# One core: the keys of a node lookup are turned on TensorE with the slots, and the marks of a tile lie in a run

## The chip, the cores and the metric

The kernel runs on one core of one Trainium2 chip. The metric is the device time of one execution in microseconds (us), the median of several runs. In the text PE is TensorE, DVE is VectorE, ACT is ScalarE, POOL is GpSimd and SP is SyncE, which here only issues DMAs.

## The reference

One layer of a graph network, with a normalisation behind it. There are 12,500 nodes with 32 features and 400,000 edges sorted by their destination.

```python
msg = jax.nn.relu(node_inputs[src] + edge_inputs)
agg = jax.ops.segment_sum(msg, dst, num_segments=N_NODES)
h = (1.0 + eps[0]) * node_inputs + agg
y = h @ W.T + b
x = _layernorm(x + y, axis=-1)
```

The costly part is `node_inputs[src]`: 400,000 rows of 32 floats, read at random places.

## The kernel before, in words

The edges are cut into 195 batches of 2048 (and a short first one). A batch is 16 tiles of 128 edges. The rows of its 8 first tiles are fetched by POOL with indirect DMAs (`gather_tile`, L536), one for each tile of 128 rows. The rows of the other 8 tiles are looked up on TensorE, in two stages, with the node table `xparts` held in SBUF as three bf16 parts.

- First lookup (`look_in_buckets`, L1154, tile `l`): a node's low bits are its bucket (32), the rest its place. Each source gets a slot in its bucket. Marks `oh1` (1 where a slot's place is the lane) are made by DVE (L754, two of three) and ACT (L989, L996) from `slots`, a row of 1824 numbers that every partition gets by a broadcast DMA. ACT copies the result to `table` (L964).
- Second lookup (`look_in_table`, L1173, tile `found`): marks `oh2` say which slot each of the 1024 edges wants. They are made from `keys`, 1024 numbers broadcast in the same way, by DVE (L766, three of four blocks) and ACT (L1008, L1014). A step does 4 blocks x 8 tiles x 3 parts = 96 matmuls of 128x128, each with 128 columns of marks as its weights. The marks stand edge by edge, tiles innermost, and `PITCH` is LOOK + 2 = 10, so the 128 marks of one tile lie 10 elements (20 bytes) apart.

Then DVE picks the right row out of `found` (L781), adds the edge's features for all 16 tiles (`add_rows`, L797), ACT does the relu (L979), DVE marks each edge's node in a window of 40 (L800), PE sums (L1184), and DVE adds the window to `aggX` (L824).

How slots and keys come about, for the batch two steps ahead: DVE marks buckets (L703), PE counts ranks (`count_ranks`, L1205, L1207, L1211 with the contiguous weights `before` and `ones`), DVE takes the rank (L717, L725), the key (`give_key`, L740) and the placement (L733, L745). PE fills the slots (`fill_slots`, L1220: 8 matmuls into 32 partitions of `ranks`), ACT copies them to `slot_row` (L971). SP writes key and slots to DRAM (L483, L489) and reads both back, spread over all partitions (L491, L497).

Each engine runs its own program. Nothing is scheduled: the order is that of the `step` functions, and semaphores join them. In step s PE does `look_in_buckets`, the sums of batch s-1, blocks 0 and 1 of `found`, `fill_slots` for s+2, block 2, `count_ranks` for s+3, block 3. POOL gathers batch s+3 in three turns; each turn waits until PE has come far enough in step s (`l1_ready`, `blocks_looked`), so POOL may be some two steps ahead of `add_rows`, but no more. SP's order in a step is index, key write, edges, slot write, key broadcast, slot broadcast; a wait there holds up all that is behind it.

## Time and profile before

| | |
|---|---|
| median of 3 runs | 2077.78 us (2077.75 to 2079.56) |
| the profiled execution, its own time | 2076.23 us |
| its span (first to last instruction) | 2074.0 us |
| mean granted TensorE clock | 0.995 of full |
| PE busy | 2012.9 us (97%) |
| DVE, ACT, POOL busy | 80%, 76%, 73% |
| `found` (L1173), PE busy | 1241.0 us, 18720 matmuls |
| gathers (L536), POOL busy | 1517.0 us, 1565 gathers |

Matmuls are pipelined: a row of the timeline that holds n of them lasts n - 1 intervals and the whole length of the last. A POOL row is POOL's own part of one gather; when the gathered rows have landed is not in it. The time between two rows of one engine that the trace puts down to nothing is called "issue". Busy shares are averages over the run.

### The profile page before, as it was taken

The page shows a single profiled execution, that of the slowest core. Times are in us where ns is not written, and L with a number is a line of the kernel's source. Part 1 is how long each engine was busy: PE and PEld are TensorE (multiplying, and loading weights), DVE is VectorE, ACT ScalarE, POOL GpSimd, SP SyncE. Part 2 cuts the span into 40 slices and gives each one's busy share as a digit, 9 for nine tenths or more (in the row PEclk, how much of TensorE's full clock was granted, in tenths as well). Part 3 has the DMA queues.
Part 4 walks back from the last instruction along what each step waited for, and adds up shares of the span by engine and source line. Part 5 has one row for each costly group of instructions (what it writes and reads, how often), then busy time and mean ns, then how long its engine had stood idle before and what let it go on. Part 6 is the DMA issues. An engine that isn't in the chain of part 4 may idle for free. (4 is left out here: it accounts for less than half of the span.)

```text
span 2074.0 us, 117127 instructions
## 1 busy us (share of the span) xinstructions
PE 2012.9 (97%) x46449; PEld 1920.2 (93%) x46449; DVE 1649.0 (80%) x4231; ACT 1566.4 (76%) x1616; POOL 1517.5 (73%) x1571
## 2 busy tenths in 40 slices
PE   2999999999999999999999999999999999999997
PEld 2899999999999999999999999999999999999994
DVE  6888888878888888877888888877888888887885
ACT  5777777777777777777777777777777777777774
POOL 6477777777777777777777777777777777777770
PEclk9999999999999999999999999999999999999998
DMA  6344444444544444444444444444444444444441
GB/s 157 86 112 109 110 111 110 113 114 115 112 111 110 110 111 110 114 112 112 116 111 110 110 110 111 114 113 112 115 112 110 109 110 111 111 115 112 115 112 35
DMA packets 236283, 228.68 MB, mean 110 GB/s; under 512 B 104218, under 2 KB 185556, under 8 KB 236062
## 3 DMA queue, kind: packets, MB, share of 16 engines
q1 hardware_dynamic: 183023, 200.99, 33.5%
q0 software_dynamic: 50080, 25.74, 12.7%
q10 hardware_dynamic: 3154, 1.60, 0.4%
q8 instruction: 17, 0.28, 0.1%
q14 instruction: 9, 0.07, 0.0%
HBM read 225.43 MB, written 2.71 MB: 110 GB/s over the span
## 5 line engine op out<-in xcount | busy, mean ns | idle before, releaser
L536 POOL DMA_INDIRECT rows_all<-in_x,index x1565 | 1517.0, 969 | 507.1 <-issue 474.0
L1173 PE MATMUL found<-table,oh 128*128 128x128 bf16 x18720 | 1241.0, 225 | 11.4 <-issue 3.1
L1173 PEld LDWEIGHTS found<-table,oh 128*128 128x128 bf16 x18720 | 1167.9, 144 | 43.6 <-issue 21.2
L1008 ACT ACTIVATE oh<-keys,minus_lanes 128x1024 bf16<-128x1024 f16 x195 | 224.2, 1150 | 310.3 <-PE found L1173 294.4
L1154 PE MATMUL l<-xparts,oh 128*57 128x96 bf16 x18720 | 436.5, 207 | 0.9 <-ACT oh L996 0.9
L1154 PEld LDWEIGHTS l<-xparts,oh 128*57 128x57 bf16 x18720 | 409.7, 108 | 14.1 <-issue 1.1
L989 ACT ACTIVATE oh<-slots,minus_lanes 128x1824 bf16<-128x1824 f16 x195 | 351.3, 1801 | 0.0
L781 DVE COPY_PREDICATED rows_all<-mask,found 128x256 f32<-128x256 uint16 x780 | 343.3, 440 | 7.6 <-issue 1.4
L964 ACT CAST table<-l 128x768 bf16<-128x768 f32 x390 | 311.1, 798 | 40.2 <-PE l L1154 26.0
L996 ACT ACTIVATE oh<-oh 128x1824 bf16<-128x1824 bf16 x195 | 335.7, 1721 | 0.0
L775 DVE TENSOR_TENSOR mask<-iota,side 128x32 f16<-128x32 f16 x195 | 37.6, 193 | 305.2 <-PE found L1173 290.1
L766 DVE TENSOR_SCALAR oh<-keys,lanes 128x1024 bf16<-128x1024 f16 x585 | 274.2, 495 | 1.1 <-PE found L1173 1.0
L754 DVE TENSOR_SCALAR oh<-slots,lanes 128x1824 bf16<-128x1824 f16 x390 | 272.5, 740 | 0.2 <-DMA slots<-slot_dram 0.2
L1184 PE MATMUL win<-onehots,relus 128*32 128x40 f32 x6250 | 238.1, 204 | 3.5 <-DVE aggX L824 3.3
L1184 PEld LDWEIGHTS win<-onehots,relus 128*32 128x32 f32 x6250 | 214.3, 112 | 17.4 <-DVE aggX L824 4.2
L1014 ACT ACTIVATE oh<-oh 128x1024 bf16<-128x1024 bf16 x195 | 206.9, 1061 | 0.0
L979 ACT ACTIVATE relus<-msg 128x512 f32<-128x512 f32 (+1 forms) x196 | 123.7, 631 | 94.8 <-DVE msg L797 94.8
L800 DVE TENSOR_TENSOR onehots<-win,rel 128x640 f32<-128x640 f32 (+1 forms) x196 | 157.3, 803 | 0.0
L797 DVE TENSOR_TENSOR msg<-rows_all,msg 128x512 f32<-128x512 f32 (+1 forms) x196 | 133.1, 679 | 0.1
L824 DVE TENSOR_TENSOR aggX<-aggX,win 32x40 f32 x391 | 73.2, 187 | 61.2 <-issue 7.8
L745 DVE TENSOR_TENSOR in_slot<-ranks,bucket 128x456 f16<-128x456 f32 x195 | 121.1, 621 | 0.0
L717 DVE TENSOR_TENSOR counts<-ob,ranks 128x256 f16<-128x256 f16 x195 | 82.2, 421 | 14.7 <-DVE rows_all L781 8.0
(126 smaller groups left out, 904.4 us busy)
## 6 DMA issues: line engine op xcount, KB each, us to landing
slots<-slot_dram SPq DMA_DIRECT2D x195, 456.0 KB
msg<-in_edge SPq DMA_DIRECT2D x390, 128.0 KB
keys<-key_dram SPq DMA_DIRECT2D x195, 256.0 KB
rows_all<-in_x,index POOLq DMA_INDIRECT x1565
index<-in_src SPq DMA_DIRECT2D x195, 4.0 KB
key_dram<-key SPq DMA_DIRECT2D x195, 2.0 KB
slot_dram<-slot_row SPq DMA_DIRECT2D x195, 3.6 KB
oh<-in_x SPq DMA_DIRECT2D x3, 512.0 KB, 6.5
```

The lines of the kernel that those rows point to most:

```text
L536: pool.indirect_dma_start(to, None, x, bass.IndirectOffsetOnAxis(indices[:, j:j + 1], 0)).then_inc(done, 16)
L754: nc.vector.tensor_scalar(oh1[:, j, :], slots[:, two, :], lanes[:, j:j + 1], None, ALU.is_equal).then_inc(oh1_ready, 1)
L766: nc.vector.tensor_scalar(key_marks(b), by_edge(keys[:, four, :]), lanes[:, b:b + 1], None, ALU.is_equal).then_inc(oh2_ready, 1)
L781: nc.vector.copy_predicated(rows[slot][:, POOLED * D:ROW].rearrange("p (t f) -> p t f", f=D), mask[:, two, :, k:k + 1].bitcast(U16).to_bro ...
L964: nc.scalar.copy(table[:, some, :], l1_all[:, :].rearrange("p (k c) -> p k c", k=KEYS)[:, some, 0:PARTS * FOUND]).then_inc(table_ready, 1)
L989: nc.scalar.activation(oh1[:, DVE_SUBS, :], slots[:, two, :], ACT.Square, bias=minus_lanes[:, DVE_SUBS:DVE_SUBS + 1]).then_inc(slots_squar ...
L996: nc.scalar.activation(at, at, ACT.Relu, scale=-2.0, bias=1.0).then_inc(oh1_act_ready, 1)
L1008: nc.scalar.activation(key_marks(b), by_edge(keys[:, four, :]), ACT.Square, bias=minus_lanes[:, b:b + 1]).then_inc(keys_squared, 1)
L1014: nc.scalar.activation(at, at, ACT.Relu, scale=-2.0, bias=1.0).then_inc(oh2_act_ready, 1)
L1154: last = nc.tensor.matmul(l1_of(g)[half * HALF:half * HALF + CAP, :, :], oh1[:, j, b * CAP:(b + 1) * CAP], xparts[:, j * EVEN + b, :, :], ...
L1173: last = nc.tensor.matmul(found[:, t * FOUND:(t + 1) * FOUND], key_marks(b)[:, :, t], table[:, b, n * FOUND:(n + 1) * FOUND],  start=(b == ...
L1184: last = nc.tensor.matmul(win_sums(g), relus[:, j, :], onehots[:, j, :], start=(j == tiles.start), stop=(j == tiles.stop - 1))
```

## The change

The marks of the second lookup are stored tile by tile: edge e of tile t stands at t * 128 + e, without padding, and a tile's weights are one run of 128. For this the keys must come in that order. DVE writes the key of a batch into the first 8 of 32 columns (the others are zero), PE turns it with one matmul against the identity into 32 partitions of `ranks`, beside the slots, and ACT copies keys and slots in one piece of 185 columns to `turned_row`. SP writes both from there; its early key write is gone. Line numbers after are 5 to 9 lower.

```diff
-        oh2 = sb("oh2", [P, KEYS, P * PITCH], BF16)
+        oh2 = sb("oh2", [P, KEYS, COLS], BF16)
...
-        key = sb("key", [P, 2, LOOK], F16)
+        key = sb("key", [P, BUCKETS], F16)
...
-        slot_row = sb("slot_row", [BUCKETS, 2, CAP], F16)
+        turned_row = sb("turned_row", [BUCKETS, 2, P + CAP], F16)
...
-        slot_ps = ranks[0:BUCKETS, 384:384 + CAP]
+        key_ps = ranks[0:BUCKETS, 256:256 + P]
+        slot_ps = ranks[0:BUCKETS, 256 + P:256 + P + CAP]
+        turned_ps = ranks[0:BUCKETS, 256:256 + P + CAP]
...
         def key_marks(b):
-            return oh2[:, b, :].rearrange("p (e t) -> p e t", t=PITCH)[:, :, 0:LOOK]
-
-        def by_edge(values):
-            return values.rearrange("p (e t) -> p e t", t=LOOK)
+
+            return oh2[:, b, :]
...
-            def spread_keys(st):
-                if has(st, 2, ROWS):
-                    r, two, four = st.s + 2, slot_of(st, 2, 2), slot_of(st, 2, RING)
-
-                    sp.wait_ge(key_ready, r + 1)
-                    sp.dma_start(key_dram[four].rearrange("(p t) -> p t", t=LOOK), key[:, two, :]).then_inc(key_written, 16)
...
                     sp.wait_ge(slots_copied, r + 1)
-                    sp.dma_start(slot_dram[four].rearrange("(b c) -> b c", c=CAP), slot_row[:, two, :]).then_inc(slots_written, 16)
+                    sp.dma_start(key_dram[four].rearrange("(t p) -> t p", p=P), turned_row[0:LOOK, two, 0:P]).then_inc(key_written, 16)
+                    sp.dma_start(slot_dram[four].rearrange("(b c) -> b c", c=CAP), turned_row[:, two, P:P + CAP]).then_inc(slots_written, 16)
+
                     sp.wait_ge(key_written, (r + 1) * 16)
...
-                    wait_count(dve, key_written, (r - 1) * 16)
+
                     dve.wait_ge(rank_ready, r + 1)
-                    nc.vector.tensor_tensor(key[:, slot_of(st, 2, 2), :], of_row(bucket, r), of_row(key_base, r), ALU.add).then_inc(key_ready, 1)
+                    nc.vector.tensor_tensor(key[:, 0:LOOK], of_row(bucket, r), of_row(key_base, r), ALU.add).then_inc(key_ready, 1)
...
-                    nc.vector.tensor_scalar(key_marks(b), by_edge(keys[:, four, :]), lanes[:, b:b + 1], None, ALU.is_equal).then_inc(oh2_ready, 1)
+                    nc.vector.tensor_scalar(key_marks(b), keys[:, four, :], lanes[:, b:b + 1], None, ALU.is_equal).then_inc(oh2_ready, 1)
...
                     wait_count(act, slots_written, (r - 1) * 16)
+                    wait_count(act, key_written, (r - 1) * 16)
                     act.wait_ge(slots_ready, r + 1)
-                    nc.scalar.copy(slot_row[:, two, :], slot_ps).then_inc(slots_copied, 1)
+                    nc.scalar.copy(turned_row[:, two, :], turned_ps).then_inc(slots_copied, 1)
...
-                                found[:, t * FOUND:(t + 1) * FOUND], key_marks(b)[:, :, t],
+                                found[:, t * FOUND:(t + 1) * FOUND], key_marks(b)[:, t * P:(t + 1) * P],
...
                     wait_count(pe, slots_copied, r)
+                    nc.tensor.matmul(key_ps, key[:, :], ident_half[:, :], start=True, stop=True)
                     for t in range(LOOK):
                         last = nc.tensor.matmul(slot_ps, placed[:, t, :], in_slot[:, t, :], start=(t == 0), stop=(t == LOOK - 1))
```

On PE, the filling of the slots in a step of the main part, between blocks 1 and 2 of `found`; before:

```order
L1173 MATMUL found<-table,oh 128x128 x23
L1220 MATMUL ranks<-in_slot,placed 32x57 [waits slots_copied,placed_ready]
L1220 MATMUL ranks<-in_slot,placed 32x57 x7
L1173 MATMUL found<-table,oh 128x128 [waits table_ready,oh2_ready]
L1173 MATMUL found<-table,oh 128x128 x23
```

and after:

```order
L1168 MATMUL found<-table,oh 128x128 x23
L1214 MATMUL ranks<-ident_half,key 32x128 [waits slots_copied,placed_ready]
L1216 MATMUL ranks<-in_slot,placed 32x57 x8
L1168 MATMUL found<-table,oh 128x128 [waits table_ready,oh2_ready]
L1168 MATMUL found<-table,oh 128x128 x23
```

The matmul with `key` stands ahead of the eight for the slots and has taken over their waits; nothing else moved on PE.

On SP, one step in the loop (`DMA` rows are issues, the bare ISA rows carry a wait); before:

```order
L465 ISA [waits rows_gathered0]
L465 DMA index<-in_src 128x8
L483 DMA key_dram<-key 128x8 [waits key_ready]
L471 REGISTER_ALU
L475 ISA [waits relu_ready]
L475 DMA msg<-in_edge 128x256
L476 ISA
L476 DMA msg<-in_edge 128x256
L489 DMA slot_dram<-slot_row 32x57 [waits slots_copied]
L490 REGISTER_ALU
L491 DMA keys<-key_dram 128x1024 [waits key_written]
L497 DMA slots<-slot_dram 128x1824 [waits slots_written]
```

and after:

```order
L464 ISA [waits rows_gathered0]
L464 DMA index<-in_src 128x8
L470 REGISTER_ALU
L474 ISA [waits relu_ready]
L474 DMA msg<-in_edge 128x256
L475 ISA
L475 DMA msg<-in_edge 128x256
L481 DMA key_dram<-turned_row 8x128 [waits slots_copied]
L482 DMA slot_dram<-turned_row 32x57
L484 REGISTER_ALU
L485 DMA keys<-key_dram 128x1024 [waits key_written]
L491 DMA slots<-slot_dram 128x1824 [waits slots_written]
```

The key write moved from ahead of the edge loads to behind them, into the group that waits for ACT's copy, directly ahead of the slot write. The edge loads now wait for nothing but the relu.

## Rows read from the trace of the kernel before

**Rows 1.** The page's busy line: busy us (share of the span) xinstructions.
```profile
PE 2012.9 (97%) x46449; PEld 1920.2 (93%) x46449; DVE 1649.0 (80%) x4231; ACT 1566.4 (76%) x1616; POOL 1517.5 (73%) x1571
```

**Rows 2.** PE's timeline, one step: start us, duration us, engine, line, operation, tiles, count.
```profile
1000.82 0.41 PE L1220 MATMUL ranks<-in_slot,placed 128*32 128x57 f16 x8
1001.15 1.67 PE L1173 MATMUL found<-table,oh 128*128 128x128 bf16 x24
1002.66 0.27 PE L1205 MATMUL ranks<-ob,before 128*128 128x256 f16 x1
...
1003.00 1.61 PE L1173 MATMUL found<-table,oh 128*128 128x128 bf16 x24
...
1007.95 3.15 PE L1173 MATMUL found<-table,oh 128*128 128x128 bf16 x48
1011.03 0.40 PE L1220 MATMUL ranks<-in_slot,placed 128*32 128x57 f16 x8
```

**Rows 3.** DVE's timeline, 1007 to 1019; in brackets idle time before, and its releaser.
```profile
1008.28 0.68 DVE L797 TENSOR_TENSOR msg<-rows_all,msg 128x512 f32<-128x512 f32 x1
...
1015.04 0.19 DVE L775 TENSOR_TENSOR mask<-iota,side 128x32 f16<-128x32 f16 x1 [1.66 <-PE found L1173]
...
1018.46 0.68 DVE L797 TENSOR_TENSOR msg<-rows_all,msg 128x512 f32<-128x512 f32 x1
```

**Rows 4.** The source view of L536: ns min/median/max; idle us before it, times.
```profile
L536 POOL DMA_INDIRECT rows_all<-in_x,index x1565: 940/944/4234, 12.2 to 2024.3; - x196
...
  issue: 474.0, 1554
```

**Rows 5.** Windows, L536 alone: from:to, length, POOL busy (count), clock, DMA.
```profile
286.20:2025.30 1739.10, 1321.58 (x1371) 1.00 0.47 111
```

**Rows 6.** POOL's timeline, 1007 to 1021.
```profile
1007.78 1.07 POOL L536 DMA_INDIRECT rows_all<-in_x,index  x1 [0.30 <-issue]
...
1017.91 1.12 POOL L536 DMA_INDIRECT rows_all<-in_x,index  x1 [0.30 <-issue]
```

**Rows 7.** POOL's timeline, 82 to 88.
```profile
82.97 0.94 POOL L536 DMA_INDIRECT rows_all<-in_x,index  x1 [0.30 <-PE l L1154]
84.22 1.15 POOL L536 DMA_INDIRECT rows_all<-in_x,index  x1 [0.30 <-issue]
85.67 1.22 POOL L536 DMA_INDIRECT rows_all<-in_x,index  x1 [0.30 <-issue]
```

**Rows 8.** DVE's timeline, 83.6 to 87.9.
```profile
83.87 0.68 DVE L797 TENSOR_TENSOR msg<-rows_all,msg 128x512 f32<-128x512 f32 x1
...
85.99 1.35 DVE L754 TENSOR_SCALAR oh<-slots,lanes 128x1824 bf16<-128x1824 f16 x2
```

**Rows 9.** POOL's timeline, 185 to 190.
```profile
185.80 0.94 POOL L536 DMA_INDIRECT rows_all<-in_x,index  x1 [0.30 <-issue]
...
188.30 1.36 POOL L536 DMA_INDIRECT rows_all<-in_x,index  x1 [0.30 <-issue]
```

**Rows 10.** DVE's timeline, 185.7 to 188.9.
```profile
185.98 0.68 DVE L797 TENSOR_TENSOR msg<-rows_all,msg 128x512 f32<-128x512 f32 x1
```

**Rows 11.** Groups by line and form, weight loads: busy us, mean ns; idle before.
```profile
L1173 PEld LDWEIGHTS found<-table,oh 128*128 128x128 bf16 x18720 | 1167.9, 144 | 43.6 <-issue 21.2 <-ACT x_turned L955 0.6
...
L1211 PEld LDWEIGHTS ranks<-pairs,ones 128*128 128x128 f16 x585 | 46.5, 99 | 2.5 <-DVE pairs L710 0.2
```

**Rows 12.** ACT's timeline, 999 to 1014.
```profile
1009.53 1.80 ACT L989 ACTIVATE oh<-slots,minus_lanes 128x1824 bf16<-128x1824 f16 x1
```

**Rows 13.** Timeline of the issues on SP's queue, 1001 to 1015.
```profile
1001.48 0.33 SPq L489 DMA_DIRECT2D slot_dram<-slot_row  x1
1001.93 0.35 SPq L491 DMA_DIRECT2D keys<-key_dram  x1
1003.59 0.32 SPq L497 DMA_DIRECT2D slots<-slot_dram  x1
```

**Rows 14.** The source view of L797: ns min/median/max, first and last start us.
```profile
L797 DVE TENSOR_TENSOR msg<-rows_all,msg x196: 315/682/693, 56.7 to 2042.0; 128x512 f32<-128x512 f32 x195, 128x160 f32<-128x160 f32 x1
```

More of the change, by code:

```diff
@@ L48, in gnn_kernel @@
     EARLY_KEYS = 2
-    PITCH = LOOK + 2
     WINDOW = 40
@@ L77, in gnn_kernel @@
     ZRING = 4
+    assert LOOK * BUCKETS <= 256 and P + CAP <= 192 and LOOK <= BUCKETS
     assert SHORT <= POOLED and WINDOW <= P and LOOK % 2 == 0
@@ L213, in gnn_kernel @@
         y_sb = xparts[0:NP, :, :, :].rearrange("p b n f -> p (b n f)").bitcast(F32)[:, 0:NT * P].rearrange("p (t c) -> p t c", c=P)
-        src_rows = oh2[:, :, :].rearrange("p b c -> p (b c)").bitcast(I32)[:, 0:2 * COLS].rearrange("p (h c) -> p h c", h=2)
+        src_rows = oh2[:, :, :].rearrange("p b c -> p (b c)").bitcast(I32).rearrange("p (h c) -> p h c", h=2)
         rel_rows = src_f[:, :, :].rearrange("p h c -> p (h c)").bitcast(F16).rearrange("p (h c) -> p h c", h=2)
@@ L500, in step @@
                 load_index(st)
-                spread_keys(st)
                 load_edges(st)
@@ L582, in _ @@
             nc.vector.memset(ones[:, :].bitcast(U16), 0x3C00)
+            nc.vector.memset(key[:, :].bitcast(U16), 0)
             nc.vector.memset(one_row[:, :], 1.0)
@@ L1007, in square_keys @@
                     wait_count(act, blocks_looked, (r - 1) * KEYS + (b + 1))
-                    nc.scalar.activation(key_marks(b), by_edge(keys[:, four, :]), ACT.Square, bias=minus_lanes[:, b:b + 1]).then_inc(keys_squared, 1)
+                    nc.scalar.activation(key_marks(b), keys[:, four, :], ACT.Square, bias=minus_lanes[:, b:b + 1]).then_inc(keys_squared, 1)
             def mark_keys(st):
```

## The prediction

> **What bounds it now.** I read the page's busy line first [rows 1]: the matrix engine (PE) 97%, its weight loads 93%, DVE 80%, ACT 76%, POOL 73%. Then PE's timeline over one step [rows 2]: from one filling of slots (L1220, 1000.82) to the next (1011.03) there is hardly a gap, so PE is a bound: 10.2 us a step. The four `found` blocks fill 1.67 + 1.61 + 3.15 = 6.4 us of it. DVE agrees from the other side: it stands idle 1.66 us before its mask, released by `found` [rows 3]. Its message sum (L797) comes at 1008.28 and 1018.46.
>
> What the page hides is POOL. 73% looks idle, but its source view [rows 4] says that of 1565 gathers 1554 follow the one before after an "issue" gap, 474.0 / 1554 = 0.305 us, the median gather being 0.944 us. That is a pitch of 1.249 us, or 9.99 us for the eight gathers of a step, and no semaphore wait to speak of. In the window 286.2 to 2025.3 [rows 5] 1371 gathers take 1739.1 us: 1.2685 each, 10.15 us a step. So POOL's floor (9.99) is only 0.16 us a step under the pace of the whole kernel. POOL is the second bound, and it is near.
>
> Where do POOL's 0.16 us go? Into one gather a step [rows 6]: that at 1007.78 takes 1.07 and that at 1017.91 takes 1.12 instead of 0.94. The first ends at 1008.85, the second at 1019.03, each 0.57 us behind the start of an L797 [rows 3]. L797 (two fp32 operands in SBUF) holds up the end of a gather that is running. This also explains how both keep one pace: POOL, being faster, creeps forward in each step until L797 pushes it back by just 0.16 us. It is locked to DVE, in the cheapest place that there is. The Trainium skill, "SBUF — State Buffer", section "SBUF: two separate sides", has the mechanism: DVE operations with two SBUF inputs or in a 2-port mode hold a port pair shared with GpSimd exclusively. It has the other blocked until DVE's end plus about 115 ns; the trace has the gather end some 0.1 us before L797's recorded end, so the rows are used here.
>
> Other offsets between L797 and the gathers cost more; the start of the run shows them. L797 at 83.87, 0.90 into the gather at 82.97: the next two take 1.15 and 1.22 [rows 7, 8], 0.21 + 0.28 = 0.49 us in all. The first is held by L797, the second by the first of the two slot marks (L754), which come 2.12 us behind L797. L797 at 185.98, 0.18 into a gather: that one is spared, but the one at 188.30 runs into L754 and takes 1.36 [rows 9, 10], 0.42 more.
>
> **The change, part by part.**
> Weights in a run. The marks of a tile, now 10 elements apart, become adjacent. The weight load of `found` takes 144 ns on average, that of `ones` (L1211, also 128x128, 16 bit, but adjacent) 99 [rows 11]. The pace of `found`: with the last matmul's own 0.22 us taken off, (1.67 - 0.22)/23 = 63 ns, (1.61 - 0.22)/23 = 60, (3.15 - 0.22)/47 = 62 ns [rows 2]. With adjacent weights five matmuls of 256 + 128 + 192 + 128 + 64 = 768 columns pass between 1002.66 and 1003.00: 0.44 ns a column, 56 ns for 128. I take 56: over 93 intervals 6 ns each, 0.56 us a step. Bounds: nothing (if the pace doesn't hang on the load) and 0.56 plus some 0.1 for the first load of each block.
> The Trainium skill speaks against this term: "TensorE: Matmul & The Clock Gate", section "Weight-path perf modes", lets the fast weight load read four chunks of 32 columns "packed or strided", for any 128 weights not in fp32. By it strided marks load as fast and the gain is nothing. The two rows, 144 and 99 ns, disagree; it stays as a rival.
> The key matmul: one more 128-column matmul a step on PE, 0.06 us. Net 0.5 us; PE's own step would be 10.15 - 0.5 = 9.65.
> DVE and ACT marks write adjacent instead of strided elements: same types and counts. No row shows adjacent marks of 1024 elements. The nearest, L754, writes 1824 adjacent ones in about 0.68 us ([rows 8]: 1.35 for two); scaled to 1024 that is between 0.38 and 0.68 us for one of the three, whichever way. I take 0; a few tenths of a microsecond of either sign have cover in DVE's 1.66 us of idle time.
> ACT's copy of the slots gets 128 more columns; L989 takes 1.80 us for 1824 [rows 12], so that is an eighth of a microsecond, behind no wait of PE's that this step shows.
> SP. The early key write and its wait go; edge loads no longer stand behind it and are issued up to 5 us earlier. In the slot chain a key write comes first: one issue more, 0.45 us (1001.48 to 1001.93), and the key broadcast now waits for the written keys, so it goes out just ahead of the slot broadcast instead of 1.66 us ahead [rows 13]. Slots are issued at 1003.59 and read by ACT at 1009.53 [rows 12]: 5.9 us for 456 KB. I take this as hidden; the keys have another whole step.
>
> **Where the gain goes.** With PE at 9.65 and POOL at 9.99 or more, POOL is the bound. Its lead is worn off first: its last gather starts at 2024.3 and the last L797 at 2042.0 [rows 4, 14], 16.8 us behind that gather's end. Landing takes 1 to 4 us (no row shows it; the nearest, the slot write, 2.1 us from issue to the wait's end [rows 13]); I take 3, so 14 us come back. Then L797 starts when the last gather has landed, not when PE lets it.
> And the lock is gone: it needs a DVE step longer than POOL's. While the lead lasts L797 slides through all offsets; after that its offset is set by the landing time, which I can't place within one pitch of 1.25 us, as it is uncertain by more than that. So I take the mean over all offsets a, from the pairs above: a from 0 to 0.30, +0.33 on average (0.42 seen at 0.18, less nearer 0); 0.30 to 0.37, nothing; 0.37 to 0.64, L797's end of 0.57 makes a - 0.37, +0.13; 0.64 to 1.25, (a - 0.68) + 0.28, from 0.24 to 0.85, +0.54 (0.49 seen at 0.90). Weighted: (0.30 x 0.33 + 0.27 x 0.13 + 0.61 x 0.54) / 1.25 = 0.37 us a step. Step: 9.99 + 0.37 = 10.36 against 10.15.
> **Sum:** 190 steps x 0.21 = +40, less 14 for the lead: +26 us. The profiled execution took 2076.2 (span 2074.0, 2.2 outside it), so it would take 2102; the median of the runs is 2077.8, 1.6 higher: 2104.
>
> **The rivals.**
> A, the above: POOL bound, lock lost. 0.60. It holds as long as the gathers are lengthened by over 0.16 + 14/190 = 0.23 us a step. Its own range is 2085 to 2134 (0.53 us of lengthening: +70 - 14).
> B, the other sign: POOL bound, but the landing puts L797 where it costs little (offset 0.30 to 0.55), lengthening 0 to 0.16. With 0.08: 190 x -0.08 = -15, -14 more: 2049, between 2034 and 2064. For it: such a stretch of offsets exists and today's lock is in it. Against: it is a fifth to a quarter of the pitch. 0.22.
> C: the weights don't gain, only the key matmul is added: 195 x 0.06 = +11, 2089. Against it, 144 and 99 ns. 0.08.
> D: gathers are not the limit (the 0.305 us gap shrinks when nothing is waited for): PE's gain arrives in full, 195 x 0.5 = 98, 1980. Against: the gap is 0.30 in every row. 0.05.
> E: the slot broadcast, behind the keys, comes late and ACT waits. It decides once its 5.9 us are used up; 0.2 us a step over that is +39, 2117. 0.05.
>
> **How the numbers follow.** The likeliest is A: 2104. Low end: B to near its floor, leaving out D, 2036; high end that of A, 2134; together some 0.15 to 0.2 left out. A measurement here can tell 0.2% (4 us). Slower: 0.53 of A, most of C and E, 0.61. Same: 0.05 of A, 0.04 of the others, 0.09. Faster: B, D and a little of A, 0.30.
>
> **What would show it.** Weight loads of `found` near 100 ns and the pace at 56 ns (C is out). PE's busy share clearly lower, with idle time at the slots' filling released by DVE, and DVE idle before L797 until gathers land (A and B; D shows neither). POOL still without waits, and the window's time per gather: about 1.295 us under A, 1.25 to 1.27 under B. The lead of the last gather over the last L797 down from 16.8 to a few us. I am wrong if the mean gather under the new offsets stays below 1.278 us, or if another engine than POOL sets the step.

## The result, and the profile after

The changed kernel takes 2138.73 us (median; 2133.16 to 2140.54 in 4 runs), the kernel before 2077.78 (2077.75 to 2079.56 in 4 runs): a ratio of 1.0286, 95% interval 1.0273 to 1.0299, so it is slower by 61 us. The forecast was 2104 us, slower by 26, in a range from 2036 to 2134.

The page of the changed kernel, its busy line and its costliest groups (line, engine, operation, tiles, count | busy us, mean ns of one | idle time before, releaser), to be laid beside [rows 1, 11]:

```profile
span 2130.9 us, 117325 instructions
PE 1952.0 (92%) x46644; PEld 1823.7 (86%) x46644; DVE 1675.9 (79%) x4232; ACT 1563.4 (73%) x1616; POOL 1587.2 (74%) x1571
...
L529 POOL DMA_INDIRECT rows_all<-in_x,index x1565 | 1586.7, 1014 | 508.2 <-issue 455.6
L1168 PE MATMUL found<-table,oh 128*128 128x128 bf16 x18720 | 1146.9, 220 | 38.4 <-DVE oh L760 20.3
L1168 PEld LDWEIGHTS found<-table,oh 128*128 128x128 bf16 x18720 | 1052.6, 98 | 81.0 <-issue 62.3
...
L791 DVE TENSOR_TENSOR msg<-rows_all,msg 128x512 f32<-128x512 f32 (+1 forms) x196 | 137.4, 701 | 193.6 <-issue 99.8
```

The gathers and the sum of the kernel before, from its page:

```profile
L536 POOL DMA_INDIRECT rows_all<-in_x,index x1565 | 1517.0, 969 | 507.1 <-issue 474.0
L797 DVE TENSOR_TENSOR msg<-rows_all,msg 128x512 f32<-128x512 f32 (+1 forms) x196 | 133.1, 679 | 0.1
```

TensorE (PE) got what the change offers: its weight loads for `found` went from 144 to 98 ns, and it is busy for 92% of a longer span. POOL's share hardly moved. What moved is the mean of its gathers, from 969 to 1014 ns. The median was 944 [rows 4]; the 70 ns over it, in eight gathers, are 0.56 us a step, where it was 25 ns, or 0.20 us.

Windows of the changed kernel, the gathers alone (from:to, length, busy and count, clock, DMA share), to be laid beside [rows 5]:

```profile
core 0: us, POOL busy (x), PEclk, DMA share, GB/s
190.00:510.00 320.00, 244.79 (x247) 1.00 0.42 113
510.00:1000.00 490.00, 377.75 (x369) 1.00 0.40 106
1000.00:1500.00 500.00, 384.19 (x381) 1.00 0.40 107
1500.00:2000.00 500.00, 384.59 (x379) 1.00 0.40 108
```

Eight gathers took 8 x 320 / 247 = 10.36 us from 190 to 510, and 10.62, 10.50 and 10.55 in the three later windows. The forecast of 10.36 is met in the first window, by luck as is told further down, and in no other.

One step of the changed kernel on POOL and on VectorE (DVE): start, length, line, operation, and in brackets the idle time before it with its releaser. They answer to [rows 3, 6]:

```profile
1009.03 0.95 POOL L529 DMA_INDIRECT rows_all<-in_x,index  x1 [0.30 <-issue]
...
1011.54 0.94 POOL L529 DMA_INDIRECT rows_all<-in_x,index  x1 [0.31 <-issue]
...
1014.04 1.36 POOL L529 DMA_INDIRECT rows_all<-in_x,index  x1 [0.30 <-issue]
```

```profile
1011.51 0.75 DVE L791 TENSOR_TENSOR msg<-rows_all,msg 128x512 f32<-128x512 f32 x1 [0.75 <-DMA rows_all<-in_x,index]
...
1013.31 0.68 DVE L760 TENSOR_SCALAR oh<-keys,lanes 128x1024 bf16<-128x1024 f16 x1
1013.90 1.28 DVE L748 TENSOR_SCALAR oh<-slots,lanes 128x1824 bf16<-128x1824 f16 x2
```

The sum (L791) now waits for the gathered rows, 0.75 us here: POOL sets the step. It starts 2.5 us after the last gather of its batch did (1009.03). The gather at 1014.04 starts inside the first slot mark (L748, 1013.90) and takes 1.36 us instead of 0.94. The next sum of this view is at 1021.92, a step of 10.41 us. Other steps lose more: in them one gather is held by the sum and the next by a slot mark.

The waits of the changed kernel (who waited for whom: us in total, times, longest), PE, DVE and then SyncE's queue:

```profile
PE ranks L1214 <- DVE in_slot L739: 101.7, 140, 11.6
DVE msg L791 <- issue: 99.8, 82, 3.5
DVE msg L791 <- DMA rows_all<-in_x,index: 93.8, 82, 1.6
```

```profile
SPq L464 <- DMA rows_all<-in_x,index: 777.9, 164, 5.8
```

The sum's 193.6 us of waiting is new (0.1 us before), and TensorE waits where the forecast had it wait, at the filling of slots (L1214), for DVE, which is late because of the sum.

### The profile page after: what moved, and what is told of

Its sections match the earlier page's. It is cut to its first block and busy times, and to the rows that moved or that the text cites. A ratio compares the mean times of both kernels' runs of the same rounds, so it can differ in the third digit from the quotient of the medians.

```text
span 2130.9 us, 117325 instructions
## 1 busy us (share of the span) xinstructions
PE 1952.0 (92%) x46644; PEld 1823.7 (86%) x46644; DVE 1675.9 (79%) x4232; ACT 1563.4 (73%) x1616; POOL 1587.2 (74%) x1571
## 2 busy tenths in 40 slices
DMA packets 211323, 228.68 MB, mean 107 GB/s; under 512 B 79258, under 2 KB 160596, under 8 KB 211102
## 5 line engine op out<-in xcount | busy, mean ns | idle before, releaser
L529 POOL DMA_INDIRECT rows_all<-in_x,index x1565 | 1586.7, 1014 | 508.2 <-issue 455.6
L1168 PE MATMUL found<-table,oh 128*128 128x128 bf16 x18720 | 1146.9, 220 | 38.4 <-DVE oh L760 20.3
L1168 PEld LDWEIGHTS found<-table,oh 128*128 128x128 bf16 x18720 | 1052.6, 98 | 81.0 <-issue 62.3
L984 ACT ACTIVATE oh<-slots,minus_lanes 128x1824 bf16<-128x1824 f16 x195 | 351.1, 1800 | 0.5 <-DMA slots<-slot_dram 0.5
L760 DVE TENSOR_SCALAR oh<-keys,lanes 128x1024 bf16<-128x1024 f16 x585 | 297.6, 535 | 1.1 <-PE found L1168 1.0
L791 DVE TENSOR_TENSOR msg<-rows_all,msg 128x512 f32<-128x512 f32 (+1 forms) x196 | 137.4, 701 | 193.6 <-issue 99.8
L748 DVE TENSOR_SCALAR oh<-slots,lanes 128x1824 bf16<-128x1824 f16 x390 | 258.9, 704 | 0.0
L794 DVE TENSOR_TENSOR onehots<-win,rel 128x640 f32<-128x640 f32 (+1 forms) x196 | 157.7, 804 | 0.0
L1214 PE MATMUL ranks<-ident_half,key 128*32 128x128 f16 x195 | 44.1, 226 | 103.6 <-DVE in_slot L739 101.7
L1214 PEld LDWEIGHTS ranks<-ident_half,key 128*32 128x32 f16 x195 | 18.1, 93 | 134.3 <-issue 113.6
```

The lines of the kernel that those rows point to most:

```text
L529: pool.indirect_dma_start(to, None, x, bass.IndirectOffsetOnAxis(indices[:, j:j + 1], 0)).then_inc(done, 16)
L748: nc.vector.tensor_scalar(oh1[:, j, :], slots[:, two, :], lanes[:, j:j + 1], None, ALU.is_equal).then_inc(oh1_ready, 1)
L760: nc.vector.tensor_scalar(key_marks(b), keys[:, four, :], lanes[:, b:b + 1], None, ALU.is_equal).then_inc(oh2_ready, 1)
L984: nc.scalar.activation(oh1[:, DVE_SUBS, :], slots[:, two, :], ACT.Square, bias=minus_lanes[:, DVE_SUBS:DVE_SUBS + 1]).then_inc(slots_squar ...
L1168: last = nc.tensor.matmul(found[:, t * FOUND:(t + 1) * FOUND], key_marks(b)[:, t * P:(t + 1) * P], table[:, b, n * FOUND:(n + 1) * FOUND], ...
```

## The experiments

The runs came in five sets, each set on one chip with runs of the kernel before beside it. In two sets the kernel before took what it took at first: 2081.1 us and 2079.0 us. In the other three it took 3085.2, 3081.5 and 3083.8 us, and two kernels that ran in both kinds of set took 924 and 1050 us more there. Those eleven runs are told in a part of their own below; where a kernel was run in both kinds of set, it is told here.

### Does POOL bind the changed kernel? One gather less a batch

Both kernels, with seven gathers a batch instead of eight (the eighth tile's rows are never fetched), everything else alike (the counts that the waits ask for follow; of each edit the lines that matter are shown):

```
-    TURNS = [(0, 3), (3, 6), (6, POOLED)]
+    GOT = POOLED - 1
+    TURNS = [(0, 3), (3, 6), (6, GOT)]
```

Changed kernel:

> The changed kernel with seven gathers a batch instead of eight: the eighth tile of POOL's half is never fetched and holds zeros, so the output is not the reference's; all other work is done. POOL's floor falls to 7 x 1.249 = 8.74 us a step. Theory (the gathers bind the changed kernel): PE's own step shows at last. In the changed kernel's early steps, before POOL binds, PE takes 9.70 us a step (9.67 three times, 9.81 once), against 10.15 before: 190 x 0.45 = 86 us under the kernel before, 1992 us (1980 to 2005). Rival (the key write in the slot chain, or DVE's in_slot behind the sum, sets the step): the time stays near 2139.

Kernel before:

> The kernel before with seven gathers a batch instead of eight (the eighth tile of POOL's half holds zeros, so the output is not the reference's). Theory (before the change PE bound and POOL only followed, locked to DVE): no gain, 2077 us (2070 to 2080). Rival (POOL held the kernel before as well): faster by more than 10 us.

Measured: the changed kernel with seven gathers 1995.73 us (1994.79 to 1996.88), 0.9591 of the kernel before (0.9576 to 0.9606); the kernel before with seven 2078.36, ratio 0.9988 (0.9978 to 0.9997). Both are as expected. One gather less is worth 3 us before and some 140 after (143 against the 2138.73 above, 136 against the 2131.54 of a later set; the changed kernel itself wasn't run in this one). TensorE's timeline of the changed kernel with seven gathers:

```profile
1001.56 0.39 PE L1219 MATMUL ranks<-in_slot,placed 128*32 128x57 f16 x8
1001.89 1.51 PE L1171 MATMUL found<-table,oh 128*128 128x128 bf16 x24
...
1008.38 2.80 PE L1171 MATMUL found<-table,oh 128*128 128x128 bf16 x47
```

There is no wait left in it. A block of 24 takes 1.51 us, (1.51 - 0.22) / 23 = 56 ns a matmul, as forecast. The two weight loads of `found` in the two seven-gather kernels, changed first:

```profile
L1171 PEld LDWEIGHTS found<-table,oh 128*128 128x128 bf16 x18720 | 1050.6, 98 | 43.0 <-issue 16.4
```

```profile
L1176 PEld LDWEIGHTS found<-table,oh 128*128 128x128 bf16 x18720 | 1168.0, 144 | 41.5 <-issue 14.4
```

So the change is worth 2078.36 - 1995.73 = 82.6 us, or 0.42 us a step, wherever the gathers leave room for it (the forecast: 0.5 net, 98 us in all). Rival C falls, and D with it, since with eight gathers none of it arrives. E falls by a row of the changed kernel's page: ScalarE's marks (L984) wait 0.5 us in all for the broadcast of the slots.

### Does VectorE lengthen the gathers? No lock left

The sum and both kinds of marks of VectorE cut to 2 elements a partition (their outputs are incomplete; instructions and waits stay; the marks of the first batch stay whole):

```
-  nc.vector.tensor_scalar(oh1[:, j, :], slots[:, two, :], lanes[:, j:j + 1], ...)
+  nc.vector.tensor_scalar(oh1[:, j, 0:2], slots[:, two, 0:2], lanes[:, j:j + 1], ...)
-  nc.vector.tensor_scalar(key_marks(b), keys[:, four, :], lanes[:, b:b + 1], ...)
+  nc.vector.tensor_scalar(key_marks(b)[:, 0:2], keys[:, four, 0:2], lanes[:, b:b + 1], ...)
-  nc.vector.tensor_tensor(msg[slot][:, got], rows[slot][:, got], msg[slot][:, got], ALU.add)
+  nc.vector.tensor_tensor(msg[slot][:, 0:2], rows[slot][:, 0:2], msg[slot][:, 0:2], ALU.add)
```

> The changed kernel with the sum and both kinds of marks of VectorE cut to 2 elements (results incomplete). Theory, where the kernel before takes about 2080 us: no lock is left, the step is 8 x (0.944 + 0.305) = 9.99 to 10.05 us and the time 2036 to 2045 us. Rival (what is over 9.99 is landing and not locks): 2100 or more. Where the kernel before takes about 3082 us: as in the last two sets, 3078 to 3087.

The changed kernel itself, beside it:

> The changed kernel itself, once more. Where the kernel before takes 2078 to 2084 us: 2133 to 2142. Where it takes about 3082, as in the last two sets: there TensorE's own pauses bind and the gathers have time to spare, so the lengthening costs nothing and only TensorE's gain of 0.46 us a step is left: 3040 to 3060 us. Rival: the change is slower there too, 3090 or more.

Measured, on the same chip: 2033.85 us (2030.3 to 2035.63), ratio 0.9782 (0.9766 to 0.9798), against 2131.54 (2130.61 to 2132.11), ratio 1.0253 (1.0236 to 1.027), for the changed kernel; each lies some 2 us under its expected range. POOL in the kernel without locks, one group of the page and a window of the gathers:

```profile
L529 POOL DMA_INDIRECT rows_all<-in_x,index x1565 | 1485.7, 949 | 507.2 <-issue 423.8 <-PE found L1168 51.1 <-PE l L1149 20.8
```

```profile
1000.00:1500.00 500.00, 378.07 (x401) 1.00 0.42 113
```

8 x 500 / 401 = 9.98 us a step: the floor of 9.99 that [rows 4] gave. The two kernels are 98 us apart, 0.51 us a step, and 97.0 of it is in the length of the gathers: POOL was busy for 1582.7 us with them in the changed kernel beside it, and for 1485.7 here. That is the lengthening by VectorE's work on large tiles, measured without any rule about offsets; it doesn't tell the sum's part from the marks'.

### Which operation, and what about it? The sum in four pieces

```
-  nc.vector.tensor_tensor(msg[slot][:, got], rows[slot][:, got], msg[slot][:, got], ALU.add).then_inc(sums_ready, 1)
+  for k in range(4):
+      piece = slice(k * width, (k + 1) * width)
+      added = nc.vector.tensor_tensor(msg[slot][:, piece], rows[slot][:, piece], msg[slot][:, piece], ALU.add)
+      if k == 3:
+          added.then_inc(sums_ready, 1)
```

> The changed kernel with the sum done in four instructions of 128 elements, one right behind the other. Where the kernel before takes about 2080 us: 2085 to 2115 if GpSimd gets the port between two of them, 2135 to 2160 if the lock lasts as long as the four together. Where it takes about 3082: 3038 as in the last set, and the same as the changed kernel beside it.

Measured: 2115.17 us (2114.42 to 2116.67), ratio 1.0176 (1.0159 to 1.0193), at the edge of the lower case: 16 us less than the changed kernel beside it, although VectorE works longer. Its timelines, POOL and then VectorE:

```profile
1712.73 1.02 POOL L529 DMA_INDIRECT rows_all<-in_x,index  x1 [0.30 <-issue]
1714.05 0.94 POOL L529 DMA_INDIRECT rows_all<-in_x,index  x1 [0.30 <-issue]
1715.30 1.35 POOL L529 DMA_INDIRECT rows_all<-in_x,index  x1 [0.30 <-issue]
```

```profile
1712.64 0.90 DVE L794 TENSOR_TENSOR msg<-rows_all,msg 128x128 f32<-128x128 f32 x4 [0.71 <-DMA rows_all<-in_x,index]
...
1715.16 1.28 DVE L748 TENSOR_SCALAR oh<-slots,lanes 128x1824 bf16<-128x1824 f16 x2
```

The four pieces begin 0.09 us ahead of the gather at 1712.73 and last until 1713.54; the gather takes 1.02 us, 0.08 more than 0.944. A whole sum 0.08 us ahead of a gather costs it 0.50 (the next experiment shows the row). So GpSimd gets in between two pieces. The gather at 1715.30 meets the slot mark and loses 0.41, as in the changed kernel.

Added up over all steps from 600 us on, with the lengthening of the gather that runs when the sum starts and of the one behind it put down to the sum, and the rest to the marks: the changed kernel beside it loses 0.22 us a step to the sum and 0.34 to the marks, the one with pieces 0.05 and 0.41. The pieces take away 0.17, and the marks, which now fall elsewhere, take 0.07 of it back; 0.1 us over the 145 steps from there on is 15 us, and 16 were measured.

### Can TensorE be slowed just enough? Seven useless matmuls a step

The changed kernel, with seven matmuls of 128x128 added to each step ahead of the first block of `found`, so that TensorE needs about as long as before and the lead comes back:

```
+  for _ in range(7 if b == 0 else 0):
+      nc.tensor.matmul(found[:, 0:P], ident_half[:, :], ident_half[:, :], start=True, stop=True, ...)
```

> The changed kernel with seven useless 128x128 matmuls added on PE in every step, ahead of block 0 of found. They cost 7 x 0.056 = 0.39 us a step, so PE's step becomes 9.70 + 0.39 = 10.09 us, just above POOL's floor of 10.01. Theory (the loss comes from DVE and POOL no longer being locked together): the lock is back, gathers are lengthened by some 0.1 us a step instead of 0.54, and the kernel gets faster by added work: 2078 - 190 x 0.06 = 2066 us (2058 to 2074). Rival (the change itself costs the time, on SP, ACT or DVE): added work gains nothing, 2139 or more.

Measured: 2122.67 us (2115.33 to 2130.6), ratio 1.0201 (1.0174 to 1.0228). The expectation failed. Adding work to TensorE doesn't cost (2138.73 and 2131.54 us without it, in other sets), so it isn't the bound, but the lock didn't hold. From 107 to 804 us a step took 10.11 us, 0.12 over the floor of 9.99, but by the trace the gathers lost 0.39 us in each, and so the lead was used up at 804 us. In 30 of these 69 steps a gather met the second key mark (L760), which began some 0.08 us ahead of it, and lost 0.27. That by itself is 0.12 us a step; the rest went to the sum and the slot marks, for after such a mark the sum was out of its cheap place (behind the one at 480 us it began 0.13, 1.03 and 0.62 us into a gather, where it had begun 0.42 to 0.57 into one for five steps). From 804 us on it is the changed kernel again:

```profile
1015.66 1.44 POOL L529 DMA_INDIRECT rows_all<-in_x,index  x1 [0.30 <-issue]
1017.40 1.21 POOL L529 DMA_INDIRECT rows_all<-in_x,index  x1 [0.30 <-issue]
```

```profile
1015.58 0.69 DVE L791 TENSOR_TENSOR msg<-rows_all,msg 128x512 f32<-128x512 f32 x1 [0.86 <-DMA rows_all<-in_x,index]
...
1017.71 1.36 DVE L748 TENSOR_SCALAR oh<-slots,lanes 128x1824 bf16<-128x1824 f16 x2
```

This is the dear case that the changed kernel falls into as well: a sum 0.08 us ahead of a gather makes it end at 1017.10 (0.50 us late), and the next gather runs into the slot mark (0.27 us): 0.77 us in one step.

### Can the sum be put in a cheap place? The wait for the gathers moved

The changed kernel, with VectorE waiting for the gathers ahead of the giving of keys and the marking of buckets, and the sum behind these:

```
   place_sources(st)
   find_rank(st)
-  add_rows(st)
+  meet_gathers(st)
   give_key(st)
   mark_buckets(st)
+  add_rows(st)
```

> The changed kernel, with DVE's wait for the gathers moved from the sum (add_rows) ahead of give_key and mark_buckets, and the sum behind these two. Same work. Once POOL binds, the sum then starts 0.43 us later behind the landing, 0.34 into a gather instead of 1.16, and the slot marks follow it 1.69 us later instead of 2.12. Theory (what counts is where the sum and the slot marks fall in the gathers): by the rules read from the first trace the lengthening falls from 0.6 to some 0.1 us a step; 2078 + 190 x (10.11 - 10.15) - 15 = 2055 to 2065 us (2050 to 2090, as the marks of the keys aren't in the rules). Rival (POOL's pitch does not depend on the place of these operations): 2139.

Measured: 2159.32 us (2154.0 to 2161.6), ratio 1.0367 (1.0353 to 1.0381). Wrong, and on the other side. POOL and VectorE:

```profile
1004.47 1.20 POOL L529 DMA_INDIRECT rows_all<-in_x,index  x1 [0.30 <-issue]
1005.98 1.40 POOL L529 DMA_INDIRECT rows_all<-in_x,index  x1 [0.30 <-issue]
```

```profile
1003.70 0.17 DVE L734 TENSOR_TENSOR key<-bucket,key_base 128x8 f16 x1 [1.47 <-DMA rows_all<-in_x,index]
...
1004.17 0.68 DVE L794 TENSOR_TENSOR msg<-rows_all,msg 128x512 f32<-128x512 f32 x1
```

The sum follows the end of its wait by 0.47 us, as meant. But the rows now land later: with eight gathers counted off per step, from 500 us on the sum starts on average 4.7 us after the last gather of its batch did, not 2.5 + 0.5. The time of landing isn't a constant that one may add to. SyncE issues the edge loads only once the gathers have landed (L464 waits for them), here as in the changed kernel. What moved nearer are the broadcasts of keys and slots: SyncE issues them 3.6 and 2.9 us ahead of the last gather of a batch in the changed kernel, and 1.3 and 0.9 us ahead of it here. Whether they delay the rows wasn't tried. The sum, 0.30 us ahead of the gather at 1004.47, costs it 0.26, and the next one meets the slot mark and loses 0.46: 0.72 us in the step.

### Eleven runs beside a kernel of 3082 us

In three sets the kernel before took some 1000 us more than in the others, on three other chips. The changed kernel as it is wasn't run in them. One step of TensorE there, in the kernel with the short sum (run short_sum_c):

```profile
1501.77 0.49 PE L1149 MATMUL l<-xparts,oh 128*57 128x96 bf16 x7
1502.75 0.20 PE L1149 MATMUL l<-xparts,oh 128*57 128x96 bf16 x1 [0.49 <-issue]
1503.47 1.82 PE L1149 MATMUL l<-xparts,oh 128*57 128x96 bf16 x75 [0.51 <-issue]
...
```

In the middle of a loop over one kind of matmul, all of whose operands are there, TensorE stops for half a microsecond, again and again. Its granted clock is 0.94 on average instead of 0.995, and its busy time rises as well, to 2320.5 us (1952.0 in the changed kernel at first). A window of that kernel's gathers (264 of them where the changed kernel has 381) shows POOL at half load:

```profile
1000.00:1500.00 500.00, 251.98 (x264) 0.96 0.29 75
```

There the gathers bind nothing, a step takes 8 x 500 / 264 = 15.2 us, and what they lose to a lock costs nothing. So the times of these runs can't speak to the theory. What was expected of each, and what came:

The sum alone cut to 2 of 512 elements (messages incomplete), three times: 3060.51 us, ratio 0.9922 (0.991 to 0.9935); 3051.24, 0.9902 (0.9884 to 0.9919); 3054.95, 0.9901 (0.9884 to 0.9917).

> The changed kernel with only the sum (add_rows) cut to two elements, so the output is not the reference's; the marks stay whole, and come 0.57 us sooner behind the landing. Theory (the sum lengthens the gather that it meets, 0.25 to 0.47 us a step of the 0.6, and the marks the rest): the rules give about 10.2 us a step instead of 10.53, 2087 us (2055 to 2110). Rival (only the marks matter): 2139; rival (only the sum matters): 2030.

> The changed kernel with the sum of the gathered rows and the edges cut to 2 of its 512 elements (so its messages are incomplete), and nothing else. Theory (the gathers bind, and VectorE's locks lengthen them, the sum's share being about 0.3 of the 0.54 us a step): the step falls from 10.53 to about 10.24 us and the time to 2083 us (2060 to 2095); the marks' share stays. Rival one (the sum's wait for landing is itself the bound, whatever its length): no change, 2130 to 2140. Rival two (TensorE binds): no change.

> The changed kernel with the sum cut to 2 of its 512 elements (messages incomplete), all marks whole. Of the 98 us between the changed kernel (2132) and the one without locks (2034), the sum should hold somewhat more than half: 2075 to 2090 us, and the marks the rest. Rival (the marks hold nearly all, the sum only shifts them): 2110 to 2130. Rival (the sum holds nearly all): 2040 to 2055.

Sum and marks cut to 2 elements: 3084.2, 0.9993 (0.9984 to 1.0002), and 3082.59, 1.0007 (0.9997 to 1.0017).

> The changed kernel with the sum (add_rows) and all of DVE's slot and key marks cut to two elements each after the first row, so the output is not the reference's; every instruction, wait, DMA and matmul stays. Theory (these operations of DVE lengthen the gathers): no gather is lengthened, POOL goes at 8 x 1.249 = 9.99 us a step, and with 2.4 us from the last gather to the last sum and 33 us behind it the span is 84.2 + 190 x 9.99 + 8.7 + 2.4 + 33 = 2027, the time 2030 us (2022 to 2042). Rival (gathers are slowed by the DMA queues, which stay as they are): 2139.

> The changed kernel with the sum and both kinds of marks of VectorE cut to 2 elements (results incomplete). Theory: no lock is left, the gathers keep their unlengthened pace of 8 x (0.944 + 0.305) = 9.99 us, the step is 10.0 to 10.05 and the time 2036 to 2045 us. It cannot come to 1996 (TensorE's own step of 9.70, as with seven gathers a batch) unless the pace of the gathers is itself a matter of VectorE. Rival (what is over 9.99 is landing and not locks): 2100 or more.

Eight useless matmuls instead of seven: 3140.54, 1.0177 (1.0163 to 1.019).

> The changed kernel with eight useless matmuls a step on PE instead of the seven of pad7: PE's step 9.70 + 0.45 = 10.15 us, that of the kernel before. pad7 lost its lock in one step of four, where the second marking of keys began 80 ns before a gather instead of 73. Theory (the lock of POOL to DVE is what the kernel before has and the changed one lacks): with the old margin of 0.14 us the lock holds for most of the run, lengthening 0.15 to 0.3 us a step, 2078 us (2074 to 2100), 40 to 60 us faster than the changed kernel by added work. Rival (pad7 was faster by something else, and each matmul more costs its 0.056 us): 2123 + 195 x 0.056 = 2134.

The kernel before with its marks laid out tile by tile, and the keys written to memory in that order by the transfer itself (`key_dram[four].rearrange("(t p) -> t p", p=P)`, so 1024 pieces of two bytes): 4692.82, 1.5214 (1.518 to 1.5248).

> The kernel before with the marks in a run, but without the turning of keys on PE: DVE's keys go to DRAM early, as before, by a DMA of single elements (1024 of two bytes) that puts them in the order of the tiles. SP's order is that of the kernel before. Theory (PE's gain alone unlocks POOL, whatever the keys' way): PE's step is 9.64, POOL binds, and the time is that of the changed kernel or between it and 2090, depending on where the landing puts the sum (2085 to 2145). Rival (the loss is in the keys' way through ACT and SP): PE's gain comes through, 2040 or less.

The sum in four pieces: 3038.73, 0.9862 (0.9845 to 0.9878).

> The changed kernel with the sum done in four instructions of 128 elements, one right behind the other. If the lock is held for one instruction at a time and GpSimd gets in between two of them, a gather is lengthened by at most 0.2 us where it was by up to 0.56, and the time is 2085 to 2115 us. If GpSimd does not get in between, the lock lasts as long as the four together, which are some 0.1 us longer than the one: 2135 to 2160 us. Where TensorE binds nothing of it would show: 2138.

The wait for the gathers two small operations earlier (ahead of `place_sources` and `find_rank`): 3042.57, 0.9878 (0.9862 to 0.9895).

> The changed kernel with the wait for the gathers put ahead of the placing of sources and the finding of ranks on VectorE, so that the sum starts 0.66 us later behind the last gather than in the changed kernel, with the same work. Theory (where in a gather the sum falls decides): it falls at about 0.57 us of the next but one gather instead of 1.16 of the next, where the rule read from the trace gives 0.2 us instead of 0.28 to 0.5: step 10.35 to 10.45, time 2105 to 2125 us. Rival (landing moves with the order of work, as it did when two more operations were put ahead of the sum): 2140 to 2170.

The sum in 4 pieces, each slot mark of VectorE in 3 and each key mark in 2: 3100.4, 1.0049 (1.0032 to 1.0066). With slot marks in 6 and key marks in 4: 3105.16, 1.0071 (1.0054 to 1.0088).

> The changed kernel with the sum in 4 pieces, each slot mark of VectorE in 3 (608 elements) and each key mark in 2 (512), all work done. If the length of the one instruction that covers a gather's last part sets what it loses, the lengthening goes from 0.44 us a step (with only the sum in pieces) to 0.20 to 0.30, and the time to 2070 to 2090 us, with some 0.4 us a step more on VectorE, which has room. If the locked time in total counts: 2115 to 2130, no better than with the sum alone in pieces.

> The same with each slot mark in 6 pieces (304 elements) and each key mark in 4 (256), all work done. If the length of the one instruction counts, the lengthening falls to 0.10 to 0.25 us a step: 2050 to 2080 us, below the kernel before (2079). VectorE gets some 1.2 us a step more, to about 9.3 of 10.1; if it becomes the bound, or the fixed part of each piece locks as long as a whole one does, 2090 or more.

Three things may be noted. Less work on VectorE did not help in proportion there: with the marks cut as well as the sum, the time was 24 and 31 us longer again in the two sets that have both, which stays unexplained. The gathers still show what lengthens them. Their mean on the page is 994 ns with the sum in four pieces and the marks whole (split4), 957 and 958 with the marks in pieces too (split_432, split_464), and 951 with sum and marks cut (short_dve). A part of that is only where the marks fall, since with the marks whole and the sum cut it is 961 to 965. Like against like: a pair of slot marks that began 0.3 to 0.5 us into a gather cost it 0.33 us whole (30 pairs, short_sum_c) and 0.08 in six pieces each (27 pairs, split_464). In three pieces each the gain doesn't show: pairs that began 0.1 to 0.3 us in cost 0.34 (27 pairs, split_432), where whole ones cost 0.13 (15 pairs, split4_b). What such pieces would save where the gathers bind isn't known. And the run with the two-byte pieces (layout_only) shows the pauses at their worst. One of its waits:

```profile
PE found L1171 <- issue: 972.2, 705, 9.7
```

Against 151.5 us in the first short-sum run, TensorE stood still for 972 us in `found` without waiting for anything that the profile shows, in a kernel whose transfers have twice as many packets (411003 against 211323). What the pauses come from no run shows.

## Why the prediction was wrong, point by point

**What bounds it.** Right. POOL was the second bound at 9.99 us a step (9.98 with no locks), 0.16 under the pace of the kernel, and seven gathers a batch free some 140 us after the change and 3 before.

**The weights.** Right: 98 ns a load, 56 ns a matmul. The step of TensorE alone was put at 9.65 us; with seven gathers the whole kernel makes 7 x 500 / 362 = 9.67 us. The Trainium skill's "TensorE: Matmul & The Clock Gate", section "Weight-path perf modes", lists weights "packed or strided" for the fast load and gives no price for the strided kind; here they had one, 144 against 98 ns a load and 62 against 56 ns a matmul.

**Marks, copy, queue.** Their cost was put at nothing and they cost nothing that shows: the median key mark takes 481 ns in both kernels (the mean rose from 495 to 535), and the wider copy 289 on average where the narrower took 198, beside idle time. SyncE's chain stayed hidden. Not foreseen: its index load now waits for the gathers, 777.9 us in all, and so places the edge loads behind the landing.

**The lead.** Right: 14 us were to come back. The last gather starts at 2095.1 and the last sum at 2097.9, so 1.9 us of the 16.8 are left: 15 us.

**The lengthening of the gathers: the term that was mis-sized.** It was put at 0.37 us a step, the mean over all offsets of the sum in a gather, and is 0.54 from 1000 us on (8 x 1000 / 760 = 10.53, less 9.99). With 190 steps the difference, 0.17 us, is 32 us; the sum with it is 190 x (10.53 - 10.15) = 72, less 15: +57, and the profiled execution took 2133.2, 56.9 more than the 2076.2 of the kernel before. POOL's totals say the same: it was busy with gathers for 1586.7 us where it had been for 1517.0, and 69.7 less 15 is 55. The step that failed is the one from a landing that can't be placed to the mean over all offsets.

Of the time while the lead lasts the prediction said that the sum slides through all offsets, and the 10.36 us in the window from 190 to 510 look like a proof of it. They aren't; the agreement is luck. From 192 to 357 us the sum alternates between two places, 0.03 to 0.09 us into a gather, where a slot mark costs 0.42, and 0.57 to 0.71 into one, for 0.21 to 0.31. That is 0.35 us a step. POOL and VectorE in two steps that follow each other:

```profile
269.22 0.94 POOL L529 DMA_INDIRECT rows_all<-in_x,index  x1 [0.30 <-issue]
...
271.71 1.36 POOL L529 DMA_INDIRECT rows_all<-in_x,index  x1 [0.30 <-issue]
...
278.37 1.17 POOL L529 DMA_INDIRECT rows_all<-in_x,index  x1 [0.30 <-issue]
```

```profile
269.30 0.68 DVE L791 TENSOR_TENSOR msg<-rows_all,msg 128x512 f32<-128x512 f32 x1
...
271.58 1.28 DVE L748 TENSOR_SCALAR oh<-slots,lanes 128x1824 bf16<-128x1824 f16 x2
...
278.97 0.68 DVE L791 TENSOR_TENSOR msg<-rows_all,msg 128x512 f32<-128x512 f32 x1
```

From some 430 us on the sum was tied to the landing, 2.5 us after the start of the last gather (the forecast: 3 us after its end), and 2.5 us is two pitches less a little. That puts the sum at or just ahead of the start of a gather, so that a step falls to one of two cases: 0.42 us, where the sum spares the gathers and a slot mark holds one (1014.04 above), or 0.77, as in the rows of the seven-matmul run. Of the 141 steps from 600 to 2090 us, 59 lost 0.4 us and 72 lost 0.7 to 0.8. The prediction's own rule has both, 0.42 for the start of the pitch and (1.17 - 0.68) + 0.28 = 0.77 for its end; 0.54 lies between. Only at the very edge it was wrong: it gave less than 0.42 next to 0 and 0.82 for 1.22, and the runs show 0.42 at both. With the landing fixed, the mean over all offsets describes no step at all. The rule was there, and a bound on it too: the row of A's own range with 0.53 us of lengthening gave 2134. With a landing given in pitches the likeliest value would have been between 0.42 and 0.77, which is 2113 to 2180 us by the same sum, and the range would have had to reach as high.

**The rivals.** A happened, just beyond the far end of its range (2134). B (a cheap offset, 2049) needed the landing in a fifth of the pitch. It had that for seven steps, from 1127 to 1188 us, when the landing took up to 3.4 us and a step lost 0.15; nothing in the kernel holds it there, and moving it by hand failed (2159). C, D and E are out by the runs above.

**What stays open.** How the lengthening divides between sum and marks is added up from the traces (0.22 and 0.34 us a step) and agrees with one run, the sum in four pieces; the run with only the short sum never came to a chip of the quicker kind, nor did those with the marks in pieces, which alone could tell whether all pieces together would beat the kernel before. Why the landing grows by some 1.7 us when the wait moves by 0.5. What the pauses of the 3082 us sets are. No kernel with all its work done beat the kernel before where that takes 2079 us.

## What to carry to other kernels

Before speeding up the engine that binds, look for the queue just under it, by its pitch and not by its busy share: POOL was 73% busy and 0.16 us a step from being the bound. When the bound moves from an engine to a chain of transfers, the phase between engines that share a port is no longer free: don't average a phase that a fixed delay will pin, but compute the cost at both ends of where the delay can fall. And try splitting a long locking instruction before moving it: here four pieces of the sum gave 16 us, and moving it lost some 20.

## What the runs showed of the hardware

- Nearly all that a gather on GpSimd loses here it loses to VectorE's fp32 sum of 128x512 and to its marks in 16 bit (128x1824, 128x1024). With these cut to 2 elements the mean gather is 949 ns; with them 1011 to 1014. What is left of VectorE's work then costs a single gather 0.17 us at most (from 190 to 2000 us). The fp32 comparison of 128x640 (L794) cost 0.01 on average where it began 0.4 us into a gather (124 times); at dear offsets it was hardly met alone.
- Where in a gather the sum begins decides. In the traces of the kernel before, the changed one and that with seven matmuls, a sum that began 0.00 to 0.35 us in cost the gather nothing, one 0.40 to 0.60 in cost it 0.04 to 0.21, and one 0.10 ahead 0.47.
- A lock is held for one instruction at a time: four sums of 128x128 back to back, beginning 0.09 us ahead of a gather, cost it 0.08 us, and one of 128x512, 0.08 ahead, 0.50. With a whole sum the edge is sharp: 0.03 us ahead of a gather (1011.51 and 1011.54 above) it is the sum that takes 0.75 us instead of 0.69, and the gather loses nothing. The page "SBUF — State Buffer" of the Trainium skill, section "SBUF: two separate sides", gives a shared pair of ports to whichever engine starts first, for its whole instruction. The pieces agree with a lock that ends with the instruction. That the first to start keeps it isn't so here, as a sum that begins inside a running gather holds up that gather's end [rows 3, 6].
- The gap of 0.30 us between two gathers and their 0.944 us stay the same whether POOL is ahead by 17 us or is the bound; a saturated POOL shows as "issue" gaps and not as a wait.
- The same program took 2079 to 2081 us in two sets and 3082 to 3085 in three, each set on a chip of its own, and the kernels of the latter show half-microsecond pauses of TensorE in the middle of matmuls that wait for nothing (849 of them in `l` in short_sum_c, 480.0 us).
